# Fused adaLN transformer block on one core: the first chunk's norm taken at once, the norms of chunks three and four moved into the loop's first two slots

## What is computed

```python
mod = silu(c) @ wmod                       # six vectors per batch: sa, ca, ga, sb, cb, gb
h = layernorm(x) * (1 + ca) + sa           # the input norm: what the change moves
x = x + ga * attention_stack(h)            # 8 layers, see below
h = layernorm(x) * (1 + cb) + sb
x = x + gb * mixture_of_experts(h)         # 2 shared units, 8 experts, top 2

# one layer of the attention stack
Q = elu(x @ Wq + bq) + 1;  K = elu(x @ Wk + bk) + 1;  v = x @ Wv + bv
KV = sum_s(K * v);  Ksum = sum_s(K)        # per batch and feature
V = Q * KV / (Q * Ksum + 1e-6)
x = layernorm(gelu(V @ Wo + bo) + x) * ln1_s + ln1_b
h = gelu(x @ Wf1 + bf1)                    # 128 -> 512
x = layernorm(gelu(h @ Wf2 + bf2) + x) * ln2_s + ln2_b
```

## Time and profile before

| | |
|---|---|
| median of three runs | 550.27 us (549.25 to 550.69) |
| time of the profiled execution | 552.4 us |
| its span (first to last instruction) | 550.4 us |
| busy: PE, DVE, ACT, POOL | 524.2, 434.3, 380.9, 246.8 us |
| mean granted PE clock | 0.991 |

### The profile page before, as it was taken

One profiled execution on the slowest core, in us unless ns is written; L12 is line 12 of the kernel. 1 busy time (PEld: TensorE's weight loads), 2 busy tenths in 40 slices (PEclk: granted clock), 3 DMA queues, 4 the chain that ended last, 5 costly groups with the idle time before them and its releaser, 6 DMA issues.

```text
span 550.4 us, 7866 instructions
## 1 busy us (share of the span) xinstructions
PE 524.2 (95%) x1892; PEld 295.7 (54%) x1892; DVE 434.3 (79%) x1659; ACT 380.9 (69%) x532; POOL 246.8 (45%) x281
## 2 busy tenths in 40 slices
PE   3789999999999999999999999999988999999996
PEld 2345555555555555555555555555544345766663
DVE  5758888888888888888788888888885858888854
ACT  2757788887877888878777888887765545564642
POOL 2234454444554544455545544545442343555451
PEclk9989999999999999999999999999988999999999
DMA  8200010001000000100010010001000000000000
GB/s 249 72 0 17 5 38 2 14 5 38 14 5 19 19 14 5 38 14 5 7 31 14 5 38 14 0 5 38 0 2 0 0 2 1 19 1 21 0 20 20
DMA packets 15910, 11.21 MB, mean 20 GB/s; under 512 B 8189, under 2 KB 13693, under 8 KB 15893
## 3 DMA queue, kind: packets, MB, share of 16 engines
q1 hardware_dynamic: 15316, 10.42, 6.9%
q10 hardware_dynamic: 576, 0.60, 0.3%
HBM read 9.96 MB, written 1.05 MB: 20 GB/s over the span
## 4 chain that ended last, share of the span: by engine, by line
PE 87%; DVE 5%; issue 3%; POOL 2%; DMA 1%; ACT 0%; SPq 0%; DVEq 0%; POOLq 0%
PE bank L369 19%; PE bank L360 15%; PE bank L284 12%; PE bank L357 6%; PE bank L384 5%; PE bank L320 4%; PE bank L317 4%; PE bank L466 3%; PE bank L468 3%; PE bank L329 2%; PE bank L323 2%; PE bank L469 2%; PE bank L470 2%; PE bank L506 2%; PE bank L525 2%
## 5 line engine op out<-in xcount | busy, mean ns | idle before, releaser
L369 PE MATMUL bank<-hid,wf 128*128 128x512 f32 x256 | 125.6, 593 | 0.0
L360 PE MATMUL bank<-x,wf 128*128 128x512 f32 x192 | 94.1, 599 | 0.0
L720 POOL TENSOR_TENSOR rsD<-veD,c_half 128x4 f32<-128x4 f32 x32 | 38.4, 1200 | 121.7 <-DVE veD L809 121.7
L632 ACT ACTIVATE hid<-bank,vbf 128x512 f32<-128x512 f32 x128 | 80.9, 688 | 6.8 <-PE bank L360 3.9
L369 PEld LDWEIGHTS bank<-hid,wf 128*128 128x128 f32 x256 | 45.6, 189 | 46.5 <-ACT hid L632 27.2
L733 POOL TENSOR_TENSOR y<-g,xs 128x512 f32<-128x512 f32 x32 | 40.7, 1273 | 39.2 <-ACT g L638 39.2
L681 ACT ACTIVATE sg<-bank 128x512 f32<-128x512 f32 x40 | 23.9, 597 | 46.8 <-PE bank L470 35.0
L360 PEld LDWEIGHTS bank<-x,wf 128*128 128x128 f32 x192 | 37.2, 194 | 33.4 <-issue 22.7
L786 POOL TENSOR_TENSOR sc_lo<-sc,sc_hi 128x512 fp32r<-128x512 f32 x28 | 36.4, 1301 | 39.6 <-ACT sc_hi L689 36.2
L796 DVE BATCH_NORM_STATS2 stB<-bank 128x6 f32<-128x128 f32 x128 | 28.5, 285 | 31.9 <-PE bank L284 31.9
L720 POOL TENSOR_TENSOR rsB<-veB,c_half 128x4 f32<-128x4 f32 x32 | 32.6, 1020 | 42.3 <-DVE veB L809 42.3
(11 more groups left out here) (148 smaller groups left out, 1100.4 us busy)
## 6 DMA issues: line engine op xcount, KB each, us to landing
wf<-in_w_f SPq DMA_DIRECT2D x16, 256.0 KB, 2.7
wu<-in_w_unit SPq DMA_DIRECT2D x10, 192.0 KB
wqkv<-in_w_qkv SPq DMA_DIRECT2D x7, 192.0 KB, 2.3
x<-in_x SPq DMA_DIRECT2D x4, 256.0 KB, 6.3
out<-ot SPq DMA_DIRECT2D x4, 256.0 KB, 2.9
wo<-in_w_o SPq DMA_DIRECT2D x8, 64.0 KB, 1.8
wmod<-in_w_mod ACTq DMA_DIRECT2D x1, 384.0 KB, 4.1
vln<-in_v_ln SPq DMA_DIRECT2D x16, 1.0 KB, 1.7
```

Source lines behind the costliest of these rows:

```text
L360: mm = nc.tensor.matmul(ps_ff[j][:], wf1[:, j * P:(j + 1) * P], x2[(c - 2) % CH][:], start=True, stop=True)
L369: mm = nc.tensor.matmul(ps_f0[:], wf2[:, j, :], hid[:, j, :], start=(j == 0), stop=(j == FJ - 1))
L632: nc.scalar.activation(hid[:, j, :], ps_ff[j][:], ACT.Gelu_apprx_tanh, bias=vbf1[:, j:j + 1]).then_inc(h_ready, 1)
L720: nc.gpsimd.tensor_tensor(rs[buf(k, n)][:], ve[buf(k, n)][:], c_half[:], ALU.pow).then_inc(rstd_ready[k], 1)
```

## The change

Three things move; no arithmetic and no instruction is added or dropped.
- DVE's work before slot 0 is now: statistics of chunk 0, modulation, norm of chunk 0, statistics and norm of chunk 1. The statistics of chunk 2 and chunk 3 go to the place "after the last norm" of slots 0 and 1, and their norms to "within the first norm" of the same slots. POOL's `rstd("I", 2)` and `rstd("I", 3)` go to "end" of slots 0 and 1.
- PE transposes chunk 1 at "middle" of slot 0, chunk 2 at "start" of slot 1 and chunk 3 at "start" of slot 2. ACT writes `xs[1]` at "middle" of slot 0, `xs[2]` and `xs[3]` at a new place, "before the gelus", of slots 1 and 2.
- The output projection of item 0 waits for three chunks of `x_ready` and not for four. `slots` takes one set of extras for each of the first three slots.

```diff
-        def slots(eng, one_slot, extra=None):
-            one_slot(0, 0, 0, extra)
-            for s in range(1, CH - 1):
-                one_slot(s, s % CH, s // CH)
+        def slots(eng, one_slot, *extras):
+            extras = extras + (None,) * (CH - 1 - len(extras))
+            for s in range(CH - 1):
+                one_slot(s, s % CH, s // CH, extras[s])
...
-                        pe.wait_ge(x_ready, CH)
+                        pe.wait_ge(x_ready, CH - 1)
...
-            slots(pe, slot, {"middle": rest_to_fm})
+            slots(pe, slot, {"middle": lambda: first_to_fm(1)}, {"start": lambda: first_to_fm(2)},
+                  {"start": lambda: first_to_fm(3)})
...
+                run(extra, "before the gelus")
                 for j in range(FJ):
...
-            slots(act, slot, {"middle": rest_of_first_norm})
+            slots(act, slot, {"middle": lambda: first_norm(1)}, {"before the gelus": lambda: first_norm(2)},
+                  {"before the gelus": lambda: first_norm(3)})
...
-            for c in range(CH):
-                rstd("I", c)
+            rstd("I", 0)
+            rstd("I", 1)
...
-            slots(pool, slot)
+            slots(pool, slot, {"end": lambda: rstd("I", 2)}, {"end": lambda: rstd("I", 3)})
...
-            for c in range(CH):
-                dve.wait_ge(ld["x0"][c], 16)
-                stats("I", c, x0[:, c], EPS_MOD)
-                if c:
-                    normalize("I", c - 1, x0[:, c - 1])
-                if c == 1:
-                    modulation()
-            normalize("I", CH - 1, x0[:, CH - 1])
...
+            first_stats(0)
+            modulation()
+            first_norm(0)
+            stats_and_norm(1)
...
-            slots(dve, slot)
+            slots(dve, slot, {"after the last norm": lambda: first_stats(2), "within the first norm": lambda: first_norm(2)},
+                  {"after the last norm": lambda: first_stats(3), "within the first norm": lambda: first_norm(3)})
```

More of the change, by code:

```diff
@@ L299, in first_to_fm @@
                 transposes([ps_f0, ps_f1, ps_b, ps_d][c], rows_of("I", c), to_fm["I"])
-            def rest_to_fm():
-                for c in range(1, CH):
-                    first_to_fm(c)
             first_to_fm(0)
@@ L595, in first_norm @@
                 ev.then_inc(x_ready, 1)
-            def rest_of_first_norm():
-                for c in range(1, CH):
-                    first_norm(c)
             first_norm(0)
@@ L840, in modulation, with first_stats, first_norm, stats_and_norm @@
                                                op0=ALU.add, op1=ALU.mult).then_inc(mod_done, 1)
-            for c in range(CH):
+            def first_stats(c):
                 dve.wait_ge(ld["x0"][c], 16)
                 stats("I", c, x0[:, c], EPS_MOD)
-                if c:
-                    normalize("I", c - 1, x0[:, c - 1])
-                if c == 1:
-                    modulation()
-            normalize("I", CH - 1, x0[:, CH - 1])
+            def first_norm(c):
+                normalize("I", c, x0[:, c])
+            def stats_and_norm(c):
+                first_stats(c)
+                first_norm(c)
+            first_stats(0)
+            modulation()
+            first_norm(0)
+            stats_and_norm(1)
             def slot(s, c, l, extra=None):
```

## The result

| | before | changed |
|---|---|---|
| median of eight runs each | 549.99 us (549.25 to 552.91) | 555.11 us (550.92 to 556.31) |
| profiled execution, its span | 552.4, 550.4 us | 555.0, 553.0 us |
| mean granted PE clock there | 0.991 | 0.983 |
| first `ff1` (item 0) | 34.84 us | 37.37 us |
| from there to the end of the span | 515.56 us | 515.63 us |

The ratio is 1.0074 (95% interval 1.0048 to 1.0100): slower, as forecast. The time lies above my range, which ended at 554.0.

What follows compares the result with a forecast made beforehand. PE bounds the kernel (87% of the span), so only the first ff1's start counts. Terms +0.14, +0.8, +1.0, -0.44, +0.85 = +2.3 us: 554.7 as a profile, 552.6 as median; range 551.0 to 554.0.

Steps and rivals of the forecast that it cites:

- `xs` ahead of `wo`: Item 0's wo must also wait for xs[2], ready at 26.2 us: wo starts at 26.25 against 24.35, +1.9.
- two norms in a row: Norm of chunk 3 between rk and the norm of B, 1.11 us less 0.25 hidden: +0.85.
- the transposes of chunk 3: Ahead of ff1 in slot 2, they hide behind DVE's x2: 0.
- 1.52 + 0.8 + 1.0 - 0.44: Chunk 2's terms: statistics ahead of elu_q_sb, later vt, xs[2] behind it, less g1's former wait for the table alone.
- DVE's earlier entry: DVE reaches slot 0 by about 14.5 us, so mq starts at 17.59 and not 18.97: 1.38 us gained.
- "The runs' median, 550.27, lies 2.1 below it, so I forecast 552.6": Last step: profiled execution 552.4 plus 2.3 gives 554.7 us, lowered by 2.1 to a median of 552.6.
- "I take neither": PE clock unknowns left at 0: low at wo +0.8, at chunk 2's transposes +0.5; high at y1's transposes -0.5.
- the rival I gave 0.16: PE at 1.2 GHz from about 26 us, wo ends at 28.2, all behind 0.8 to 1.3 later: 553.4 to 553.9; chance 0.16.
- "I take 0 for `xs[0]`": Start: norm of chunk 0 at 9.5 to 9.6 us, at most 0.1 earlier, so xs[0] and slot 0's projections don't move.
- the rival that makes the change faster: Start waits for x0[1]: each us of landing after 8.06 delays only before; landing at 12 us gives 548.6; chance 0.07.
- up to 0.5 us on this rule at `rsB`: POOL's rsB is held by the norm of chunk 3, delaying the norm of B: +0.5, 553.1; taken as 0, chance 0.10.
- The 0.63 us: Earlier trace: DVE's wait after a norm beside POOL's power of chunk 3, against 0.25 for rsB; cited for mutual blocking.

Runs made afterwards that it cites:

- late3: The changed kernel, but chunk 2 is done as before and only chunk 3 is moved: 549.82 us, ratio 0.9993 to before.
- after_again: The changed kernel run once more, nothing altered, beside new runs of the kernel before: 553.16 us, ratio 1.0042.
- norm_first: The changed kernel with the norm of chunk 0 ahead of the modulation: 552.05 us, ratio 1.0030 to before.
- best: split3 with the norm of chunk 0 ahead of the modulation, without idle matmuls: 545.39 us, ratio 0.9907 to before.
- a_start: The kernel before with only modulation and norm of chunk 0 put ahead of the statistics of chunk 1: 551.47 us, ratio 1.0011.
- own_bank: The changed kernel, but chunk 2 is transposed into ps_y behind wo, which needs no wait for xs[2]: 552.12 us, ratio 1.0044 to before.
- pool_first: The changed kernel, but POOL does the power of chunk 2 ahead of kpos and qk in slot 0: 553.56 us, ratio 1.0049 to before.
- split3: late3 with statistics of chunk 3 at the end of slot 0 and its norm behind elu_q_sb in slot 1: 549.10 us, ratio 0.9981 to before.
- before_again: The kernel before once more, unaltered, for a second profile: 552.58 us (one run).
- before_fill: The kernel before with unread matmuls filling PE's waits in slots 1 and 2 and two slots behind the loop: 547.76 us, ratio 0.9947.

## Why the prediction was wrong

**The steps held, in part by luck.** From `mq` to `ff1` every row of the changed profile lies within 0.6 us of its forecast, with the releasers named: `xs` ahead of `wo`, the table load behind it, 1.40 us of waiting for POOL, two norms in a row, nothing from the transposes of chunk 3 (35.98 to 37.37 is 1.39 us) and nothing from the late `hid`. Profile against profile the change costs 2.6 us where I had 2.3. But two errors cancel in this: the start came 0.5 us early and the slow `wo` cost 0.9. The second pair of profiles, without the slow `wo`, is 1.7 us apart. late3 confirms the sizes for chunk 2: my terms are 1.52 + 0.8 + 1.0 - 0.44 = 2.9 us, against a gain of 1.38 by DVE's earlier entry, and without them `ff1` comes 2.8 us earlier.

**The step that failed: from the profile to the median.** "The runs' median, 550.27, lies 2.1 below it, so I forecast 552.6": this takes the changed kernel's median to lie as far below such a profile as that of before. It didn't: its profiled run (555.00) is its median (555.11). Forecast as a profile, 552.4 + 2.3 = 554.7 us, it is met within 0.4. The 2.1 us fit clock and landing in the one profiled execution of before, which had lost 3.2 us behind `ff1` to the clock; the changed kernel's had lost the same 3.2, and six of its first eight runs have the mean clock of that execution (0.983) or a lower one. The range had no term for this. The runs of the kernel before differ by up to 7 us: the mean time at a clock of 0.986 lies 4.1 above that at 0.997, and runs with the same mean clock differ by up to 4 us. With the clock held the spread is 1.2. So a median of eight leaves a microsecond open.

**The clock was not 0.** "I take neither" for PE's lower level at `wo`. The changed kernel's first eight runs had a mean clock of 0.983 in five, one had 0.982, and its profile shows `wo` at 2.04 us: +0.9, the rival I gave 0.16. In after_again PE waited as long and `wo` still ran in 1.10:

```profile
24.07 0.66 PE L284 MATMUL bank<-ident,hf 128*128 128x128 f32 x4 [1.41 <-DVE hf L814]
25.93 1.10 PE L380 MATMUL bank<-vt,wo 128*128 128x512 f32 x2 [1.20 <-ACT xs L590]
```

So it is a chance of each run, but one that this order opens: the levels 0.983 and 0.982 came in 7 of 20 runs of the changed kernel and in none of 116 of before, where `wo` has a single wait of 1.18 us in front. That the low `wo` is what makes these runs is argued from two profiles (of the changed kernel at 0.983 and of norm_first at 0.982), not shown for each.

**The start was not 0, in either direction.** "I take 0 for `xs[0]`" rested on one landing of `x0[1]`, 8.06 us, and one end of the modulation matmuls, 8.42. These ended at 7.85 and 7.98 in the profiles of the changed kernel, so that its norm of chunk 0 started at 9.00 and 9.13, 0.6 and 0.4 us earlier than before. And I priced only a later landing, as the rival that makes the change faster. The load also lands earlier (7.15), and then the order before starts that norm at 8.69: the gap is 3.0 us there and 1.9 with the load at 7.72; about 0.5 of that difference is the landing.

**What is left.** Of the 5.1 us between the medians, the waits are 1.8 us (`ff1` of the second profiles, load at 8.0) to 3.0 (clock held, load at 7.15), and the slow `wo` is 0.9. The remaining 1.2 to 2.4 I can't assign. The clock of the hand-over, worth up to 3.2 us, would be enough for it if the changed kernel's runs lost it there more often than those of before beside them, whose clocks are not on record. The twelve later runs, with a gap of 2.3, speak for chance; it was not shown for the first eight. All 20 runs of the changed kernel have a median of 554.1, against 550.5 for 116 of before.

## What to carry to other kernels

Where two steps wait for different arrivals (a load, some small matmuls), ask of each order what happens when either arrival moves both ways, and put first the step whose input is ready first: here the norm ahead of the modulation brought `xs[0]` 2.2 us earlier (9.33 us in best, 11.52 in after_again). Together with the fourth chunk moved into waits, which thins DVE's queue ahead of slot 0, it made the only new order that is clearly faster than before without idle matmuls (ratio 0.9907). Work moved into a pipeline slot is free only in a wait that nothing else ends; chunk 3 fitted into two of DVE's waits, and chunk 2, which the next slot's `wo` was waiting for, did not. A forecast from one profile should be compared with a profile, or say what that one execution had lost. And with PE waiting in a few places, hold its clock before comparing two versions: idle matmuls cut the spread of the kernel before from 7 us to 1.

## What the runs showed of the hardware

**The granted clock differs from run to run at the same work.** The same order had `wo` at 1.10 us and at 2.04. In the hand-over (398 to 430 us) the granted clock was 0.89 in both profiles of before and both of the changed kernel, 0.95 in a_start and late3, and 1.00 in own_bank, pool_first and split3, which have no idle matmuls there either. In the first profile of before PE's waits in this stretch were at most 2.07 us long. Behind `ff1` there follow 515.6 to 515.8 us at 0.89, 513.7 to 513.9 at 0.95 and 512.5 to 513.2 at 1.00.

**POOL and DVE hold each other up.** In split3 the norm of chunk 3, from SBUF to SBUF, ran beside POOL's `y1`:

```profile
25.25 2.26 DVE L815 TENSOR_SCALAR hf<-x,meanI,rsI 128x128 f32<-128x128 f32 x4
...
25.48 1.26 POOL L729 TENSOR_TENSOR y<-g,xs 128x512 f32<-128x512 f32 x1 [2.13 <-ACT g L632]
```

It took 2.26 us, where it takes 1.11 alone, while POOL's addition kept its 1.26. The Trainium skill (Advanced Engine Details and Errata, section "VectorE Performance Modes") says that two-port operations of DVE and operations of GpSimd block each other; the trace agrees, and in this pair it is DVE that pays. late3 has a second case: beside the same `y1` (25.02, 1.30 us) a small operation of the statistics took 1.23 us instead of 0.16; it ended at 26.33, just as `y1` did (26.32):

```profile
25.10 1.23 DVE L798 SCALAR_TENSOR_TENSOR sqI<-stI 128x4 f32<-128x4 f32 x1
```

Beside POOL's small power it is otherwise: the norm kept its 1.11 us, and the power took 1.12 instead of 1.01 (late3, 13.33 and 13.41). The 0.63 us that I read in the earlier trace rows as half a microsecond of this came again in before_again and before_fill, but in late3 and best DVE waited only 0.20 us in the same situation, so its cause is open. For the changed kernel I had set up to 0.5 us on this rule at `rsB`; there the norm of B followed the norm of chunk 3 without a gap (33.56 + 1.09, then 34.57), so nothing was lost.
